# Two layers of Mamba and expert blocks on one core: later low parts, sums in fours, border loads moved

## The chip, the cores and the metric

The kernel runs on one core of a Trainium2 chip. Its time is the device time of one execution in microseconds, the median of several runs. The core has five engines that run side by side, each in its own order: TensorE (PE in the profile; its weight loads are PEld), VectorE (DVE), ScalarE (ACT), GpSimd (POOL) and SyncE (SP), which issues most transfers. They wait for each other through semaphores. PSUM has eight banks of 128 x 512 numbers.

## The reference, cut to what matters

```python
x = L0_attn_x                                  # (8, 256, 128)
xn = layernorm(x)
s = mamba0(xn)                                 # 16 states a channel
g = silu(moe0(xn))                             # 8 experts, the best one for each token
x = x + s * g
xn = layernorm(x)
s = mamba1(xn)                                 # 256 channels, 4 heads, 16 states
g = silu(moe1(xn))                             # all 8 experts for each token, mixed
x = x + s * g

# mamba: h = exp(delta * A) * h + delta * B * u      (a scan over the 256 tokens)
#        y = sum over the 16 states n of h[n] * C[n]
# moe1:  sum over e of cw[e] * (silu(x @ w_gate[e]) * (x @ w_up[e])) @ w_down[e]
```

All of it is in float32.

## The kernel before

The eight sequences are worked on in four pairs; a pair is 512 tokens and fills a PSUM bank's width. Layer 0 runs for all four pairs (0 to 3), then layer 1 for all four. The two layers meet at about 258 us, and this place is called the border here.

**The order of work** is written out by hand in slots. Every pair has 32 slots (UNITS), so layer 0 has slots 0 to 127. Each engine has a function `slot0` (layer 0) and `slot1` (layer 1) that issues what stands in its lists for the slot: `now(LIST, s)` gives the indices whose entry is s. Engines do not meet at slots: each goes through its own list as fast as its waits on semaphores allow, and in order, so that what stands behind a waiting instruction waits too. SyncE goes through the same slots with its transfers.

**A chunk** g of layer 0 is one state n of one pair, 64 in all, 16 a pair. `CH0` gives its slot: every second one in pairs 0 to 2. ScalarE forms its decay four chunks ahead (`decay0`), VectorE multiplies the drive by B (`drive0`, slot CH0) and scans over the tokens (`scan0`, one slot later, four state buffers in a ring), and GpSimd multiplies the state by C (`multiply0`, line 1293; VectorE does the first ten). B and C of a chunk come by one broadcast transfer from a row in memory into one of six places (`load_cb0`, lines 570 to 575), once the product that last read the place is done. TensorE sums the products over the states in a bank: `sum_product` (line 1911) multiplies the product by the identity, one matmul pair each (float32 matmuls are issued as two). `GROUP_OF` (line 104) says how many chunks GpSimd adds up itself before TensorE sums: two in pair 1, else one. In a group the first product goes to its buffer, each further one to `addend`, and an addition (line 1313) puts it on top. At the end of a pair VectorE forms y = x + sum (`tail`, step y, line 935), TensorE transposes it, VectorE takes mean and variance, GpSimd the root, VectorE the shift, ScalarE normalises, TensorE transposes back (step yn) and multiplies by the output weights. These steps stand in the slots 36 to 47 after the pair's start (`DVE_TAIL` and its likes).

**Beside it** in layer 0, 15 blocks of 256 tokens sorted by expert go through moe0 in slots 18 to 81: TensorE turns a block, ScalarE takes it, TensorE multiplies up, ScalarE takes the relu, TensorE multiplies down, ScalarE takes it out, SyncE stores it (`UP_AT` and the lists made from it). GpSimd gathers the weights of a block (`load_pack`) and later the results by token (`fetch`).

**Gate weights of layer 1** are multiplied in three passes of a fast format: for expert e SyncE loads 256 KB into one of two stages (`load_gate`, line 549), ScalarE copies the high part at slot `SPLIT_AT[e]` = 30 + 8e (`split_high`, line 1444), VectorE subtracts to get the low part at `SPLIT_LOW_AT[e]` (`split_low`, line 741). A stage is loaded again once its low part is done, so the load of e waits for low part e-2:

```python
                if e >= 2:
                    sp.wait_ge(wl_ready.sem, wl_ready.at0(0, e - 1))
```

**Layer 1** needs at its start: the mixing weights of each expert, spread over the partitions (`load_cw`, line 612: 256 KB for one expert, in the two halves of `cwb`, which layer 0 uses for a chunk's B and C until chunk 52), with which GpSimd weighs the tokens for the up product (`weigh_tokens`, line 1369); the first four chunks' B and C (`load_cb1`, line 577, two transfers of 256 KB each); and the next pair's tokens (`load_x`, line 563), whose statistics VectorE takes in slot 1 of layer 1, while pair 0 is still being worked on. In `weigh_tokens` of pair 0 and expert 0 GpSimd follows right behind its last product of layer 0. `up1` on TensorE (line 2019) reads the weighed tokens. The last steps of layer 0 on VectorE are the gate of pair 3 (`gate0`, line 958), then the delta of layer 1 (line 885), the first drive and the y of pair 3.

Of the kernel before, what the change touches and what calls it, by code (L numbers as in the profile page):

```python
# [35 lines left out]
PAIRS = B // NB  # L36
TT = T // 128
E, FT = 8, 4
UNITS = E * FT
# [52 lines left out]
XW_SLOT = 30  # L92
SPARED = 4
FIRST_GATES = [125, 127]

CH0 = [UNITS * i + (2 * c if i < PAIRS - 1 else int(1.5 * c)) for i in range(PAIRS) for c in range(N)]
CHUNKS1 = [c if c < 8 else c - 1 for c in range(C1)]
# [3 lines left out]

PLACE = [k % SIX for k in range(UNITS - FT)] + [0, 1, 4, 5]
SUM_LAG1 = 4
GROUP_OF = [2 if i in (1,) else 1 for i in range(PAIRS)]
GROUPS0 = [list(range(N * i + k, N * i + k + GROUP_OF[i])) for i in range(PAIRS) for k in range(0, N, GROUP_OF[i])]
GROUP0 = {g: n for n, group in enumerate(GROUPS0) for g in group}
SUM0_AT = [CH0[group[-1]] + (4 if len(group) > 1 else max(3, 5 - group[0] % N) if group[0] >= N else 3) for group in GROUPS0]
# [25 lines left out]
ROWS_AT = 18  # L133
PACKS = 3
SPLIT_AT = [30 + 8 * e for e in range(E)]
SPLIT_LOW_AT = [at + 4 for at in SPLIT_AT]
GATHER_AT = [80, 88, 96, 115]
TANH_AT = [85, 93, 102, 120]
GATE_AT = [87, 95, 104, 122]
# [26 lines left out]
def cb_before(g):  # L166

    earlier = [n for n in range(min(g, PAIRS * N)) if CB_OF[n] == (CB_OF[g] if g < PAIRS * N else g - PAIRS * N)]
    return earlier[-1] if earlier else None
# [13 lines left out]
def now(slots, u):  # L183

    if isinstance(slots, dict):
        return slots.get(u, "").split()
    return [c for c, at in enumerate(slots) if at == u]
# [111 lines left out]
def build(nc, x, out, x1, crow, cwrow, sorted_in, sorted_out, w):  # L299
    ctx = ExitStack()  # L300
    with ctx:
# [244 lines left out]
        def _(sp):  # L546
            tokens = lambda ap, i: ap[i * T:i * T + T, :].rearrange("(k p) d -> p k d", p=128)

            def load_gate(e):

                if e >= 2:
                    sp.wait_ge(wl_ready.sem, wl_ready.at0(0, e - 1))
                if e == 0:
                    sp.wait_ge(cv_ready.sem, cv_ready.at0(0, 1))
                sp.dma_start(stage[:, e % 2, :], w["Wg"][e]).then_inc(stage_in[e].sem, 16)
# [4 lines left out]
            def load_wu(e):  # L560
                sp.dma_start(wu[:, e, :], w["Wu"][e]).then_inc(wu_in.sem, 16)

            def load_x(j):
                sp.wait_ge(xn_ready.sem, xn_ready.at1(j, 0))
                sp.wait_ge(x_out.sem, x_out.at0(j + 1, 0))
                sp.dma_start(xt[:, :, :], tokens(x1, j)).then_inc(x_in.sem, 16)

            def load_cb0(g):

                if g % N == 0:  # L570
                    sp.wait_ge(rows_out[0].sem, rows_out[0].at0(g // N, 32))
                if cb_before(g) is not None:
                    sp.wait_ge(state_used.sem, state_used.at0(0, cb_before(g) + 1))
                src = crow[(g // N) % 2, 0, g % N:g % N + 1, :, :].rearrange("n k t -> n (k t)")
                sp.dma_start(cb_pair(g).rearrange("p k t -> p (k t)"), src.to_broadcast((128, 2 * T))).then_inc(cb0_in[CB_OF[g]].sem, 16)
# [21 lines left out]
            def load_block(b):  # L597

                if b == 0:
                    for k in range(TT):  # L600
                        sp.wait_ge(scattered[k].sem, scattered[k].at0(0, 16 * PAIRS))
                if b >= 2:
                    sp.wait_ge(blk_turned.sem, blk_turned.at0(0, b - 1))
                src = sorted_in[BLOCK * b:BLOCK * b + BLOCK, :].rearrange("(k p) d -> p k d", p=128)
                sp.dma_start(blk_x[:, b % 2, :, :], src).then_inc(blk_in[b % 2].sem, 16)

            def store_block(b):
                sp.wait_ge(blk_out_ready.sem, blk_out_ready.at0(0, b + 1))
                dst = sorted_out[BLOCK * b:BLOCK * b + BLOCK, :].rearrange("(k p) d -> p k d", p=128)
                sp.dma_start(dst, blk_out[:, b % 2, :, :]).then_inc(blk_out_done[b % 2].sem, 16)  # L610

            def load_cw(j, e):

                if j == 0 and e == 0:
                    sp.wait_ge(state_used.sem, state_used.at0(0, max(g for g in range(PAIRS * N) if CB_OF[g] == ROWS) + 1))
                if j > 0 or e >= CWR:
                    sp.wait_ge(xw_ready.sem, xw_ready.at1(j, e - CWR + 1))
                if e == 0:
                    sp.wait_ge(cw_out.sem, cw_out.at1(j, 16))
                src = cwrow[j % 2, e:e + 1, :].to_broadcast((128, T))  # L620
                sp.dma_start(cwb[:, e % CWR, :], src).then_inc(cw_in[e % CWR].sem, 16)

            def send_cw(j):
                sp.wait_ge(*use1(head_read, j, "cwT"))
                sp.dma_start(cwrow[j % 2, :, :], cwT[:, :]).then_inc(cw_out.sem, 16)
# [31 lines left out]

            for s in range(PAIRS * UNITS):
                i, u = divmod(s, UNITS)
                for e in now(SPLIT_AT, s + 10):  # L660
                    if e >= 2:
                        load_gate(e)
                for g in range(CB_RING, PAIRS * N):
                    if s == CH0[cb_before(g)] + (4 if g < 3 * N else 3):
                        load_cb0(g)
                for b in now(LOAD_AT, s):
                    load_block(b)
                for b in now(STORE_AT, s):
                    store_block(b)
                if u == ROWS_AT and i + 1 < PAIRS:  # L670
                    send_rows(i + 1, 0, 0)
                for step in now(ACT10 if i == PAIRS - 1 else {}, u):
                    if step == "cwT":
                        send_cw(0)
                    if step in ("row0", "row1"):
                        send_rows(0, 1, int(step[3]))
                if s == UP_AT[-1] + 2:
                    load_residual(0, 0)
                for j in now(GATED_AT, s - 3):
                    send_out(j, 0)  # L680
                    load_residual(j + 1, 0)
                if s == GATED_AT[0] + 5:
                    load_x(0)

                for e in range(2, E):
                    if s == 3 * UNITS + 4 + e:
                        load_wu(e)
                if s == GATED_AT[1] + 8:
                    sp.wait_ge(x_out.sem, x_out.at0(2, 0))
                    load_wu(0)  # L690
                    load_wu(1)
                if s == DOWN_AT[-1] + 6:
                    sp.wait_ge(blk_down.sem, blk_down.at0(0, BLOCKS))
                for e in range(E):
                    if s == (DOWN_AT[-1] + 6 + e if e < 6 else 3 * UNITS + 2 + e):
                        if e == 6:
                            sp.wait_ge(yT_ready.sem, yT_ready.at0(3, 0))
                        load_wd(e)
            for i in range(PAIRS):
                last = i == PAIRS - 1  # L700
                if i > 0:
                    load_cw(i, 1)
                for c in range(ROWS):
                    load_cb1(i, c)
                if i == 0:
                    load_cw(0, 0)
                    load_x(1)
                    load_cw(0, 1)
                for u in range(UNITS):
                    if u == LATE + 1 and i + 2 < PAIRS:  # L710
                        load_x(i + 2)
                    if u == (LATE if i else FIRST_LATE):
                        send_out(i - 1 if i else PAIRS - 1, int(i > 0))
                        if i == PAIRS - 1:
                            sp.wait_ge(x_out.sem, x_out.at0(PAIRS, 0))
                        load_residual(i, 1)
                    for step in ([] if last else now(ACT1, u)):
                        if step == "cwT":
                            send_cw(i + 1)
                        if step in ("row0", "row1"):  # L720
                            send_rows(i + 1, 1, int(step[3]))
                    for c in now(CHUNKS1, u - 1):
                        if c + ROWS < C1:
                            load_cb1(i, c + ROWS)
                    if u % FT == 0 and u // FT + CWR < E:
                        load_cw(i, u // FT + CWR)
                    if u == XW_SLOT - 1 and not last:
                        load_cw(i + 1, 0)
# [5 lines left out]
        def _(dve):  # L734
# [234 lines left out]
            def slot0(s):  # L969
# [13 lines left out]
                for k, name in pair_tail(DVE_TAIL, DVE_TAIL_LAST, s):  # L983
                    tail(k, name)
                for e in now(SPLIT_LOW_AT, s):
                    split_low(e)
# [762 lines left out]
        def _(pe):  # L1749
# [228 lines left out]
            def slot0(s):  # L1978
# [5 lines left out]
                for k, name in pair_tail(PE_TAIL, PE_TAIL_LAST, s):  # L1984
                    tail(k, name)
                if s in FIRST_GATES:
                    gate1(0, FIRST_GATES.index(s))
                for b in now(TURN_AT, s):
# [208 lines left out]
```

## Time and profile before

| what | value |
|---|---|
| median of 3 runs | 694.93 us (692.76 to 696.48) |
| the profiled execution, its own time | 695.81 us |
| span of its profile | 694.0 us |
| TensorE busy | 585.4 us (84%) |
| VectorE busy | 575.8 us (83%) |
| GpSimd busy | 532.7 us (77%) |
| ScalarE busy | 456.4 us (66%) |
| granted TensorE clock, mean | 0.963 of 2.4 GHz |
| transfers of SyncE's queue | 130.74 MB, 66.6% of the 16 engines' time |

The span goes from the first to the last instruction; the run's own time holds what lies around it as well. Busy shares are means over stages that have different limits: what bounds a stage is read from the stretches and from the engines' rows in time. In a row in time the bracket gives how long the engine was idle just before, and the instruction whose end released it. Several like instructions in a row are merged into one line with their count.

### The profile page before, as it was taken

How to read it: one execution, taken by the hardware profiler on the slowest of the kernel's cores; microseconds unless marked ns; L12 is line 12 of the kernel's file. 1: busy time of each engine (PE TensorE's matmuls, PEld its weight loads, DVE VectorE, ACT ScalarE, POOL GpSimd, SP SyncE). 2: the span in 40 equal slices, each digit the busy share in tenths (PEclk: the TensorE clock that was granted, in tenths of full speed). 3: DMA queues.
4: the chain of work that ended last, by engine and by line, in shares of the span. 5: the costliest groups of instructions: out<-in, count | busy, mean ns of one | idle time of the engine just before them, and what ended most of it. 6: DMA issues, size and time to landing. Idle time of an engine off the chain costs nothing. (4 is left out here: it accounts for less than half of the span.)

```text
span 694.0 us, 8481 instructions
## 1 busy us (share of the span) xinstructions
PE 585.4 (84%) x2135; PEld 339.7 (49%) x2135; DVE 575.8 (83%) x906; ACT 456.4 (66%) x723; POOL 532.7 (77%) x431
## 2 busy tenths in 40 slices
PE   4656888899745966889999799998799999899997
PEld 2412667786413423544444454444454544566674
DVE  6899819677788987997988979888989788898995
ACT  4655466877834666856787655886765887776660
POOL 3456356785785575988899799999799999799991
PEclk9999899999877988999999999999999999999999
DMA  8096896898796677677557686767676867678870
GB/s 267 17 322 229 291 296 207 286 288 294 218 306 238 224 193 183 177 201 189 153 158 198 177 203 198 189 160 190 175 197 185 208 168 192 173 204 215 221 197 15
DMA packets 71216, 142.25 MB, mean 205 GB/s; under 512 B 8352, under 2 KB 37088, under 8 KB 71168
## 3 DMA queue, kind: packets, MB, share of 16 engines
q1 hardware_dynamic: 67984, 130.74, 66.6%
q0 software_dynamic: 3184, 10.98, 4.7%
q8 instruction: 17, 0.28, 0.2%
q14 instruction: 31, 0.25, 0.1%
HBM read 133.23 MB, written 8.45 MB: 204 GB/s over the span
## 5 line engine op out<-in xcount | busy, mean ns | idle before, releaser
L927 DVE TENSOR_TENSOR_SCAN state<-decay,bank 128x512 f32<-128x512 f32 x128 | 155.9, 1218 | 12.9 <-POOL product L1262 5.3
L2019 PE MATMUL bank<-xw,wu 128*128 128x512 f32 x256 | 133.9, 605 | 14.3 <-DVE hid L1046 11.0
L1262 POOL TENSOR_TENSOR product<-state,CB 128x512 f32<-128x512 f32 x90 | 117.0, 1300 | 16.1 <-DVE state L927 12.3
L1264 POOL TENSOR_TENSOR product<-product 128x512 f32<-128x512 f32 x90 | 119.5, 1328 | 7.1
L1671 ACT ACTIVATE sg<-bank 128x512 f32<-128x512 f32 x128 | 75.4, 597 | 67.4 <-PE bank L1909 58.8
L2037 PE MATMUL bank<-hid,wd 128*128 128x512 f32 x192 | 99.1, 597 | 7.2 <-DVE hid L1046 7.2
L1046 DVE TENSOR_TENSOR hid<-sg,bank 128x512 f32<-128x512 f32 x128 | 85.0, 666 | 22.3 <-PE bank L2019 20.6
L920 DVE TENSOR_TENSOR bank<-bank,CB 128x512 f32<-128x512 f32 x128 | 88.8, 694 | 13.4 <-DMA CB<-crow 11.5
L1921 PE MATMUL bank<-product,early 128*128 128x512 f32 x112 | 71.3, 737 | 32.8 <-POOL product L1307 13.5
L1583 ACT ACTIVATE decay<-delta,negA 128x510 f32<-128x510 f32 x128 | 82.5, 710 | 12.0 <-DVE delta L885 6.8
L1907 PE MATMUL bank<-XH,wh 128*128 128x512 f32 x128 | 74.1, 579 | 9.9 <-ACT sg L1671 3.6
L905 DVE TENSOR_TENSOR_SCAN state<-decay,bank 128x512 f32<-128x512 f32 x64 | 77.9, 1217 | 3.0
L2019 PEld LDWEIGHTS bank<-xw,wu 128*128 128x128 f32 x256 | 45.8, 192 | 64.8 <-issue 46.2
L1307 POOL TENSOR_TENSOR product<-state,CB 128x512 f32<-128x512 f32 x31 | 40.5, 1313 | 22.5 <-DVE state L905 15.7
L1591 ACT ACTIVATE decay<-delta,negA 128x510 f32<-128x510 f32 x64 | 44.9, 714 | 15.4 <-DVE state L905 13.4
L1921 PEld LDWEIGHTS bank<-product,early 128*128 128x128 f32 x112 | 22.5, 228 | 62.9 <-POOL product L1307 26.3
L2037 PEld LDWEIGHTS bank<-hid,wd 128*128 128x128 f32 x192 | 35.1, 189 | 35.7 <-issue 27.2
L1908 PE MATMUL bank<-XL,wh 128*128 128x512 f32 x128 | 50.7, 396 | 0.0
L1909 PE MATMUL bank<-XH,wl 128*128 128x512 f32 x128 | 50.7, 396 | 0.0
L1907 PEld LDWEIGHTS bank<-XH,wh 128*128 128x128 f32 x128 | 24.4, 190 | 38.1 <-ACT sg L1671 13.3
L1583 ACT ACT_TABLE_LOAD x32 | 41.1, 1283 | 0.6
L1371 POOL TENSOR_TENSOR xw<-XR,cwb 128x512 f32<-128x512 f32 x30 | 39.4, 1312 | 2.3 <-PE bank L2019 1.0
(242 smaller groups left out, 1137.3 us busy)
## 6 DMA issues: line engine op xcount, KB each, us to landing
CB<-crow SPq DMA_DIRECT2D x256, 256.0 KB, 4.1
CB<-crow SPq DMA_DIRECT2D x44, 512.0 KB
cwb<-cwrow SPq DMA_DIRECT2D x32, 256.0 KB, 4.7
szm<-crow SPq DMA_DIRECT2D x11, 512.0 KB
cwb<-crow SPq DMA_DIRECT2D x9, 512.0 KB
xw<-Wg_dram SPq DMA_DIRECT2D x8, 256.0 KB, 2.9
wd<-Wd_dram SPq DMA_DIRECT2D x8, 256.0 KB, 5.5
wu<-Wu_dram SPq DMA_DIRECT2D x8, 256.0 KB, 5.3
```

The source lines that it names most:

```text
L905: v.tensor_tensor_scan(state[:, g % RING, :], place0(g), drive, 0.0, ALU.mult, ALU.add).then_inc(state_ready.sem, 1)
L920: v.tensor_tensor(drive, dx, CB[:, c % ROWS, 1, :], ALU.mult).then_inc(drive_ready.sem, 1)
L927: v.tensor_tensor_scan(state[:, c % RING, :], decay[:, PLACE[c], :], drive, 0.0, ALU.mult, ALU.add).then_inc(state_ready.sem, 1)
L1046: v.tensor_tensor(hid[:, u % 2, :], sg[:, PLACE[u], :], bank[up_bank(i, u)][:, :], ALU.mult).then_inc(hid_ready.sem, 1)
L1262: p.tensor_tensor(addend, state[:, c % RING, :], cs, ALU.mult).then_inc(state_used.sem, 1)
L1264: ins = p.tensor_tensor(product[:, m, :], product[:, m, :], addend, ALU.add)
L1583: a.activation(by_batch(decay[:, PLACE[c], :])[:, :, 1:], by_batch(delta[:, m, :])[:, :, 1:], ACT.Exp, scale=negA[:, c:c + 1]).then_inc(de ...
L1671: a.activation(sg[:, PLACE[u], :], bank[stream_bank(u)][:, :], ACT.Silu).then_inc(silu_ready.sem, 1)
L1907: t.matmul(dst, wh[:, e, ws], XH[:, :], start=True, stop=False)
L1921: t.matmul(bank[Y_BANK][:, :], ident[:, :], product[:, PRODUCT_OF[n], :], start=(c == 0), stop=(group[-1] % N == N - 1)).then_inc(summed.s ...
L2019: t.matmul(bank[up_bank(i, u)][:, :], wu[:, e, 128 * f:128 * f + 128], xw[:, e % 2, :], start=True, stop=True).then_inc(up_ps.sem, 1)
L2037: ins = t.matmul(bank[OUT_BANK][:, :], wd[:, u, :], hid[:, u % 2, :], start=(u == 0), stop=(u == UNITS - 1))
```

## The change

Four edits, in lists and in SyncE's program:

- `GROUP_OF` is 4 instead of 2 for pair 1: GpSimd adds four products before TensorE sums them. The slot of a sum is made from the group's last chunk, as before.
- `SPLIT_LOW_AT` is nine slots behind `SPLIT_AT`, for the last expert six, instead of four.
- `load_gate(e)` stands six slots ahead of `SPLIT_AT[e]` instead of ten.
- The border's loads move into the slots of layer 0: `load_x(1)` to slot 96 + 14 = 110, `load_cw(0, 0)` and `load_cw(0, 1)` to slot 96 + 23 = 119. Before, they stood behind the first eight B and C transfers of layer 1.

```diff
+NEXT_X_AT, FIRST_CW_AT = 14, 23
...
-GROUP_OF = [2 if i in (1,) else 1 for i in range(PAIRS)]
+GROUP_OF = [4 if i in (1,) else 1 for i in range(PAIRS)]
...
-SPLIT_LOW_AT = [at + 4 for at in SPLIT_AT]
+SPLIT_LOW_AT = [at + (9 if e < E - 1 else 6) for e, at in enumerate(SPLIT_AT)]
...
             for s in range(PAIRS * UNITS):
                 i, u = divmod(s, UNITS)
-                for e in now(SPLIT_AT, s + 10):
+                for e in now(SPLIT_AT, s + 6):
                     if e >= 2:
                         load_gate(e)
...
                 if s == GATED_AT[0] + 5:
                     load_x(0)
+                if s == 3 * UNITS + NEXT_X_AT:
+                    load_x(1)
+                if s == 3 * UNITS + FIRST_CW_AT:
+                    load_cw(0, 0)
+                    load_cw(0, 1)
...
                 for c in range(ROWS):
                     load_cb1(i, c)
-                if i == 0:
-                    load_cw(0, 0)
-                    load_x(1)
-                    load_cw(0, 1)
```

## Rows read from the trace of the kernel before

**Rows 1.** Busy time by stretch: us, then per engine busy (count), PEclk, DMA share, GB/s.
```profile
99.00:160.00 61.00, 55.72 (x311) 44.83 (x310) 42.90 (x58) 46.17 (x95) 43.03 (x36) 0.94 0.84 273
...
254.00:268.00 14.00, 8.19 (x23) 3.83 (x22) 9.29 (x12) 8.61 (x14) 5.20 (x6) 0.87 0.94 222
...
285.00:370.00 85.00, 79.84 (x245) 41.13 (x244) 73.97 (x97) 62.00 (x88) 76.13 (x60) 1.00 0.69 180
```

**Rows 2.** VectorE in time, 80 to 190 us: start, us, line, operation, [idle before <- releaser].
```profile
96.46 0.69 DVE L741 TENSOR_TENSOR wl<-xw,wh 128x512 fp32r<-128x512 f32 x1 [10.80 <-ACT wh L1444]
...
99.36 0.69 DVE L935 TENSOR_TENSOR xd<-xt,bank 128x512 f32<-128x512 f32 x1 [0.24 <-PE bank L1921]
...
114.54 1.23 DVE L953 SCALAR_TENSOR_TENSOR shift_t<-mv_t,rstd_t 128x4 f32<-128x4 f32 x1 [0.38 <-POOL rstd_t L1190]
...
143.44 1.00 DVE L741 TENSOR_TENSOR wl<-xw,wh 128x512 fp32r<-128x512 f32 x1 [2.61 <-ACT wh L1444]
...
158.76 0.69 DVE L935 TENSOR_TENSOR xd<-xn,bank 128x512 f32<-128x512 f32 x1 [2.83 <-issue]
```

**Rows 3.** TensorE in time, 75 to 160 us, same columns.
```profile
98.30 1.02 PE L1921 MATMUL bank<-product,early 128*128 128x512 f32 x2
...
117.36 1.05 PE L1755 MATMUL bank<-early,wu 128*128 128x128 f32 x4 [2.77 <-ACT wu L1651]
...
137.85 3.68 PE L1810 MATMUL bank<-sg,wd 128*128 128x256 f32 x8 [1.99 <-ACT sg L1600]
...
151.68 1.02 PE L1921 MATMUL bank<-product,early 128*128 128x512 f32 x2
152.54 0.38 PE L1800 MATMUL bank<-early,hid 128*128 128x128 f32 x2
```

**Rows 4.** Who waited for whom on GpSimd, 99 to 160 us: total us, times, longest.
```profile
POOL product L1311 <- DVE state L905: 10.1, 6, 1.8
POOL product L1307 <- DVE state L905: 4.1, 1, 4.1
```

**Rows 5.** GpSimd in time, at the border of the layers.
```profile
254.18 1.26 POOL L1307 TENSOR_TENSOR product<-state,CB 128x512 f32<-128x512 f32 x1
255.40 1.25 POOL L1229 TENSOR_TENSOR sp_x<-sp_x,sp_e 128x512 f32<-128x512 f32 x1
256.62 1.25 POOL L1307 TENSOR_TENSOR product<-state,szm 128x512 f32<-128x512 f32 x1
266.50 1.09 POOL L1369 TENSOR_TENSOR xw<-XNP,cwb 128x512 f32<-128x512 f32 x1 [8.62 <-DMA cwb<-cwrow]
```

**Rows 6.** VectorE: line 958 (min/median/max ns, first and last start), and rows in time after 254 us.
```profile
L958 DVE SCALAR_TENSOR_TENSOR yfT<-yfT,sg x4: 665/768/3991, 189.8 to 254.4; 128x512 f32<-128x512 f32 x4
...
267.08 0.87 DVE L746 BATCH_NORM_STATS2 stats<-xt 128x6 f32<-128x128 f32 x4 [4.04 <-DMA xt<-x]
...
292.73 0.70 DVE L920 TENSOR_TENSOR bank<-bank,CB 128x512 f32<-128x512 f32 x1 [0.70 <-DMA CB<-crow]
...
296.34 0.70 DVE L920 TENSOR_TENSOR bank<-bank,CB 128x512 f32<-128x512 f32 x1 [1.02 <-DMA CB<-crow]
```

**Rows 7.** ScalarE in time, around 145 us and at the border.
```profile
144.99 0.38 ACT L1614 ACTIVATE hid<-bank 128x256 f32<-128x256 f32 x1 [0.52 <-PE bank L1823]
...
259.06 1.33 ACT L1583 ACTIVATE decay<-delta,negA 128x510 f32<-128x510 f32 x2 [4.66 <-DVE delta L885]
```

**Rows 8.** The border on TensorE and SyncE, and one line of the transfers (issue to landing).
```profile
267.64 2.08 PE L2019 MATMUL bank<-xw,wu 128*128 128x512 f32 x2 [3.18 <-POOL xw L1369]
...
249.38 0.32 SPq L625 DMA_DIRECT2D cwrow<-cwT  x1
...
252.85 5.00 SPq L588 DMA_DIRECT2D CB<-crow  x8
257.95 0.53 SPq L621 DMA_DIRECT2D cwb<-cwrow  x1
...
cwb<-cwrow SPq DMA_DIRECT2D x32, 256.0 KB, 4.7
```

## The prediction

> **What bounds the kernel now.** I read four views in this order. First the table of stretches [rows 1]. Between 99 and 160 us, where the second pair of layer 0 runs beside the expert blocks, TensorE is busy 55.72 of 61 us, GpSimd 43.03, VectorE 42.90: TensorE sets the pace and GpSimd has 18 us to spare. From 254 to 268 us, the border of the layers, no engine is busy much over half of the time and the transfer engines are at 0.94. In layer 1 (285 to 370 us) TensorE has 79.84, GpSimd 76.13 and VectorE 73.97 of 85 us: three engines nearly full, so there a head start lasts only if all three have it.
>
> Second, VectorE's order of work [rows 2]. The largest wait is 10.80 us, from 85.66 us on, for the high part of the first gate weights. After it VectorE does one low part, one scan and one drive, is done at 99.36-0.24 = 99.12 us, and still waits 0.24 us for TensorE's sum before it can take the first pair's y. The second wait of this kind, 2.61 us before 143.44 us, is followed by an idle time of 2.83 us before the second pair's y at 158.76 us.
>
> Third, TensorE [rows 3]. It has two waits over half a microsecond in 99 to 160 us: 2.77 us before 117.36 us (for the normalised y of ScalarE) and 1.99 us before 137.85 us (for ScalarE's turned block). One sum takes 0.86 us of it: 151.68 to 152.54 us.
>
> Fourth, the border [rows 5 to 8]. GpSimd ends its last product of layer 0 at 257.88 us and then waits 8.62 us for the mixing weights of the first expert, VectorE waits 4.04 us for the next tokens, TensorE 3.18 us for GpSimd's weighed tokens. SyncE issued the weights at 257.95 us and the tokens right behind, after eight transfers for B and C from 252.85 us on.
>
> **The change, part by part.**
>
> **Low parts later.** Low part e goes from slot 34+8e to 39+8e (92 for the last), the load of gate weights e from slot 20+8e to 24+8e (e from 2 on). Eight subtractions stay eight. Removed are the waits of 10.80 and 2.61 us [rows 2]. But VectorE then reaches the first y early and waits for TensorE's sum until 99.3 us as before: the gain there is at most the 0.24 us between 99.12 and 99.36. What is late next is that sum (slot 33), which hangs on the blocks that TensorE and ScalarE hand to each other. The second wait turns into a longer wait before 158.76 us. So I count both at 0. The cost: low(0) now stands in slot 39 between the variance of the first y and its shift. The low part takes 0.69 us (96.46 us), the slack there is the wait of 0.38 us before 114.54 us [rows 2], so 0.3 us on the chain to ScalarE's normalising and TensorE's transposes at 117.36 us. If a GpSimd addition holds the low part up as well, one GpSimd instruction more, 1.26 us [rows 5]. Bounds 0 and +1.6, and I take +0.3: one addition stood beside this place before, too, and the wait was only 0.38 us. Low(1) to low(3) stay in the pair in which VectorE waits for TensorE anyway, low(4) comes to where low(5) leaves, low(6) and low(7) move within one stretch: 0.
>
> SyncE's queue: the load of gate weights e waits for low part e-2. That wait now stands one slot behind the low part (before: two), and it blocks the load of B and C of a later chunk and a block's load behind it. For e=2 SyncE waits in slot 40 until low(0) of slot 39, which is done before 114.54 us. What stands behind it has its first reader in slot 43 (the block, turned by TensorE just ahead of its wait of 2.77 us) and slot 48 (chunk 24), at 61/32 = 1.9 us a slot 8 and 17 us behind slot 39, and a transfer of 256 KB lands in 4.7 us [rows 8]: hidden by 3 us or more. Without that cover it costs what is late of them. The high part follows its load by six slots, over 11 us: hidden.
>
> **Sums in fours.** Sums at slots 38, 46, 54 and 62 go; those at 42, 50, 58 and 66 stay. Four sums by 0.86 us are 3.4 us of TensorE [rows 3]. The first (slot 38) goes into the wait of 2.77 us behind it, and the second (slot 46) into that of 1.99 us, since ScalarE ends both. The third (slot 54) and the fourth (slot 62, at 151.68 us) stand in a stretch without a wait of TensorE, where ScalarE waits for it by only 0.52 us (144.99 us, [rows 7]) and becomes the later one if TensorE gains more: I count half of each, -0.8. Bounds: 0 (ScalarE holds all) and -3.4 (all four count). GpSimd gets four additions more, 8 to 12, at 1.26 us: 5.0 us. They lie in its 18 us of idle time, of which 10.1 and 4.1 us are waits for VectorE's states [rows 4]. With these additions it still has some 13 us. The last addition of the pair comes before TensorE gets to slot 66, so the y of the pair stays where TensorE puts it. Without that cover the additions cost their 5.0 us (the slower rival).
>
> **Border loads.** Three transfers of 256 KB move up in SyncE's order: the tokens to slot 110, the two weights to slot 119, ahead of the eight B and C transfers. The tokens pass sends and loads of rows; what they read and write was ready some ten slots before. The weights wait for their own row in memory, sent at 249.38 us, and SyncE is at slot 119 at about 252.8 us [rows 8]. They put 512 KB ahead of the first B and C, which at the 222 GB/s of this stretch [rows 1] land some 2.4 us later. If VectorE's first drive of layer 1 has nothing to spare, that is a bound of +2.4.
>
> With the weights in place by about 257.5 us (issue to landing 4.7 us in the median, [rows 8]), GpSimd goes on at 257.9 instead of 266.50 us, TensorE's first up product could start at 267.64-3.18 = 264.46 us, and VectorE saves 4.04 us. By these rows alone TensorE is the last, so -3.2.
>
> Against it stands VectorE's gate instruction, line 958 [rows 6]. All of its operands are in SBUF; it takes 0.67 us at least and 0.77 in the median, but the last one, at 254.4 us, took 3.99 us. It began while GpSimd's product of 254.18 us ran, and two instructions followed that one without a gap (255.40 and 256.62 us, [rows 5]); it ended 0.5 us behind the last, at 258.4. So VectorE did not get in between GpSimd instructions that follow each other at once. In the changed kernel two weighings of 1.09 us follow at once as well, and the gate instruction would end at about 260.5 us: +2.1 on VectorE's delta, on ScalarE's decays, which waited 4.66 us for it (259.06 us, [rows 7]), on its silus and on TensorE's gate products, behind which the first up product stands. 264.46+2.1 = 266.6 us, a gain of 1.1 instead of 3.2. Then GpSimd is no longer six microseconds behind the states; the waits of VectorE of 0.70 and 1.02 us for B and C at 292.73 and 296.34 us [rows 6], whose buffers GpSimd frees, should shrink: -1.0. Border: -2.1, bounds -4.9 (3.2 and both waits of 1.7) and +1.5.
>
> The Trainium skill, "SBUF — State Buffer", section "SBUF: two separate sides", says that VectorE and GpSimd share a pair of ports under an exclusive lock, held for one whole instruction, while the other blocks. The row above agrees that it blocks and goes further, since it lasted over three instructions. By the page's rule taken for one instruction at a time the gate instruction would be let in at 255.4 us, and the border would give the full 3.2; I go by the row.
>
> **Sum.** +0.3 - 0.8 - 2.1 = -2.6 us. The profiled execution took 695.81 us (span 694.0 and 1.8 around it), which gives 693.2; it lies 0.9 above the median of 694.93 us, so a median of 692.3 us. About 0.5%, 3.5 us, is what a measurement of this kernel tells from no change; the forecast lies just inside it.
>
> **Rivals.**
> A. The border gives all: VectorE slips in between, or the weights land just after the gate instruction. 3.2 and 1.7 us at the border, 0.5 to 1 before it: -5.4, 689.5 us. For it: 8.62 us of GpSimd idle at a place where all three later bounds gain. Against: the gate instruction of 3.99 us.
> B. The border gives nothing: B and C come late behind the weights and VectorE is held 2.1 us. 694.9 us.
> C. Slower: GpSimd becomes the bound of the second pair. Place: slots 44 to 64; price: four additions by 1.26, 5.0 us, so 699.9 us. It decides as soon as GpSimd's waits for states [rows 4] are used up, since a state buffer comes free only by its product, which then stands behind an addition. For it: product and addition are 2.5 us a chunk, and chunks come in bursts behind VectorE's waits. Against: 43.03+5.0 = 48 us of work in 61.
> D. The waits of 10.80 and 2.61 us come back in full, as the share of busy time would suggest: -10 or more, 684 us. Against: TensorE's sum at 98.30 us.
> That the move does nothing at all is B.
>
> **Chances.** Forecast (-1 to -4) 0.47, A 0.26, B 0.12, C 0.09, D 0.06. Faster by over 0.5%: A, D and the edge of the forecast, 0.41. Slower by over 0.5%: C, 0.09. Within: 0.50. The range leaves out D and most of C: 687.5 to 697.0. The forecast's own range is 690.9 to 694.
>
> **What would show it.** Right: no wait for wh, but VectorE waiting about 10 us for TensorE's sum before the first y and 5 or more before the second; 52 sums of two matmuls instead of 56; GpSimd's weighing near 258 us; the gate instruction (yfT by yfT and sg) over 5 us long; TensorE's first up product about 1 us earlier against the border's own start. Wrong: a first y well before 99 us (D), a gate instruction under 4 us (A), GpSimd without waits from 117 to 160 us (C), or a drive of chunk 0 of layer 1 waiting for its transfer (B).

## The result, and the profile after

The changed kernel takes 698.88 us in the median of 18 runs (694.47 to 703.2), the kernel before 695.17 us in the runs beside it: a ratio of 1.0053, interval 1.0034 to 1.0072. It is slower, by 3.7 us. The profiled execution took 699.40 us with a span of 697.6 us, 3.6 us over the one before.

The table of stretches of the changed kernel (us, then each engine's busy time and count, granted clock, DMA share, GB/s), against [rows 1]:

```profile
99.00:160.00 61.00, 52.39 (x292) 42.50 (x291) 43.31 (x56) 44.08 (x90) 47.73 (x39) 0.92 0.79 264
254.00:268.00 14.00, 8.47 (x12) 3.17 (x11) 11.01 (x8) 8.20 (x14) 12.00 (x11) 0.65 0.68 176
285.00:370.00 85.00, 78.88 (x242) 40.67 (x242) 73.66 (x96) 61.65 (x91) 76.47 (x60) 1.00 0.71 179
```

In the second pair TensorE is 3.3 us less busy and GpSimd 4.7 us more. That has the direction that the sums in fours ask for, but the sizes can't be read here: the line counts 19 matmuls fewer, and the sums are only 8 of them. The stretches are fixed in time, and the changed kernel runs later in them (its last gate instruction starts at 260.99 us instead of 254.43), so they hold different work, at the border above all. The loss isn't to be read from these lines. Over the whole span VectorE is busy 586.4 us, 10.6 us more than before, with 906 instructions in both kernels: some of them became longer. That alone is no loss either: the changed kernel without its later low parts (e15, e18 below) has 583.8 and 583.2 us and isn't slower than the kernel before. Which instruction became longer, and where, has to be read in time.

VectorE in time, the changed kernel (start, us, line, operation, [idle before <- releaser]; its lines stand two further down than before), against [rows 2]:

```profile
100.12 0.69 DVE L937 TENSOR_TENSOR xd<-xt,bank 128x512 f32<-128x512 f32 x1 [10.04 <-PE bank L1923]
...
111.72 0.68 DVE L743 TENSOR_TENSOR wl<-xw,wh 128x512 fp32r<-128x512 f32 x1
...
115.85 1.23 DVE L955 SCALAR_TENSOR_TENSOR shift_t<-mv_t,rstd_t 128x4 f32<-128x4 f32 x1 [0.33 <-POOL rstd_t L1192]
...
192.48 0.67 DVE L743 TENSOR_TENSOR wl<-xw,wh 128x512 fp32r<-128x512 f32 x1
193.06 1.76 DVE L960 SCALAR_TENSOR_TENSOR yfT<-yfT,sg 128x512 f32<-128x512 f32 x1
...
200.49 3.62 DVE L743 TENSOR_TENSOR wl<-xw,wh 128x512 fp32r<-128x512 f32 x1
...
214.67 3.05 DVE L756 TENSOR_SCALAR veps<-mv 128x4 f32<-128x4 f32 x1
...
221.04 0.68 DVE L937 TENSOR_TENSOR xd<-wd,bank 128x512 f32<-128x512 f32 x1
...
260.99 5.03 DVE L960 SCALAR_TENSOR_TENSOR yfT<-yfT,sg 128x512 f32<-128x512 f32 x1 [1.56 <-ACT yfT L1623]
```

GpSimd in time, the same kernel, in the third pair and at the border:

```profile
198.88 0.94 POOL L1226 DMA_INDIRECT sg<-sorted_out,slot_of  x1 [0.30 <-issue]
199.83 1.28 POOL L1309 TENSOR_TENSOR product<-state,CB 128x512 f32<-128x512 f32 x1
201.06 1.27 POOL L1352 TENSOR_TENSOR wu<-wu,xr 128x512 f32<-128x512 f32 x1
202.28 1.27 POOL L1309 TENSOR_TENSOR product<-state,CB 128x512 f32<-128x512 f32 x1
205.31 1.27 POOL L1309 TENSOR_TENSOR product<-state,cwb 128x512 f32<-128x512 f32 x1 [1.77 <-DVE state L907]
...
260.73 1.25 POOL L1309 TENSOR_TENSOR product<-state,CB 128x512 f32<-128x512 f32 x1
261.94 1.25 POOL L1231 TENSOR_TENSOR sp_x<-sp_x,sp_e 128x512 f32<-128x512 f32 x1
263.16 1.25 POOL L1309 TENSOR_TENSOR product<-state,szm 128x512 f32<-128x512 f32 x1
264.38 1.08 POOL L1371 TENSOR_TENSOR xw<-XNP,cwb 128x512 f32<-128x512 f32 x1
266.42 1.16 POOL L1371 TENSOR_TENSOR xw<-XNP,cwb 128x512 f32<-128x512 f32 x1 [0.95 <-DMA cwb<-cwrow]
```

The last low part, low(7), begins at 200.49 us inside a run of three GpSimd instructions without a gap (199.83, 201.06, 202.28 us, the last ends at 203.55) and ends at 204.11: 3.62 us instead of 0.68. The run has its gap only because GpSimd's next product waits 1.77 us (the row of 205.31 us) for a state whose scan stands behind low(7) on VectorE; before, five instructions followed each other there. Some ten microseconds later the input variance (line 756) meets the next run of the same kind. Before the change low(7) stood beside gathers, and the whole of it (194.46 to 195.14 us) lies within one of them:

```profile
193.03 0.95 POOL L1224 DMA_INDIRECT sg<-sorted_out,slot_of  x1 [0.30 <-issue]
194.28 0.94 POOL L1224 DMA_INDIRECT sg<-sorted_out,slot_of  x1 [0.30 <-issue]
```

VectorE of the kernel before, same stretch:

```profile
194.46 0.68 DVE L741 TENSOR_TENSOR wl<-xw,wh 128x512 fp32r<-128x512 f32 x1
...
202.33 0.87 DVE L958 SCALAR_TENSOR_TENSOR yfT<-yfT,sg 128x512 f32<-128x512 f32 x1 [1.77 <-ACT yfT L1621]
...
208.69 0.87 DVE L746 BATCH_NORM_STATS2 stats<-xt 128x6 f32<-128x128 f32 x4 [1.12 <-DMA xt<-x]
...
211.16 1.04 DVE L754 TENSOR_SCALAR veps<-mv 128x4 f32<-128x4 f32 x1
...
215.52 0.68 DVE L935 TENSOR_TENSOR xd<-wd,bank 128x512 f32<-128x512 f32 x1
```

Longer by the change: low(7) 2.94, the variance 2.01, the gate at 193.06 us 1.1 (0.67 before). Against that, the waits of 1.77 and 1.12 us are used up. That leaves about 3 us, and the third pair's y comes 59.67 us behind the second's instead of 56.76. Not all of it is low(7)'s: the gate takes 1.76 us in every kernel with low(6) in slot 87, and the variance takes 1.03 to 2.04 us in the kernels with low(7) in slot 90, so the 1.04 us before is the low end.

**The stages.** I cut every profile at the start of each pair's y on VectorE (line 935 or 937), and at its first `hid` of layer 1 (line 1046 or 1048). For the two kernels, in us:

| stage | before | after | difference |
|---|---|---|---|
| start to first y | 99.36 | 100.12 | +0.8 |
| first to second y | 59.40 | 61.25 | +1.9 |
| second to third y | 56.76 | 59.67 | +2.9 |
| third y to first hid | 54.24 | 52.66 | -1.6 |
| first hid to the end | 424.2 | 423.9 | -0.3 |

The differences add up to the 3.6 us but for rounding. One profile's stage scatters by 1 to 3 us; with twenty profiles of kernels that have or lack an edit, the groups below tell more than one pair does.

### The profile page after: what moved, and what is told of

Read it like the earlier page. It is cut to its first block and busy times, and to the rows that moved or that the text cites. A ratio compares the mean times of both kernels' runs of the same rounds, so it can differ in the third digit from the quotient of the medians.

```text
span 697.6 us, 8472 instructions
## 1 busy us (share of the span) xinstructions
PE 586.1 (84%) x2127; PEld 339.5 (49%) x2127; DVE 586.4 (84%) x906; ACT 456.4 (65%) x723; POOL 540.3 (77%) x435
## 5 line engine op out<-in xcount | busy, mean ns | idle before, releaser
L2021 PE MATMUL bank<-xw,wu 128*128 128x512 f32 x256 | 132.1, 598 | 13.8 <-DVE hid L1048 13.8
L1264 POOL TENSOR_TENSOR product<-state,CB 128x512 f32<-128x512 f32 x90 | 117.9, 1310 | 17.6 <-DVE state L929 13.8
L1309 POOL TENSOR_TENSOR product<-state,CB 128x512 f32<-128x512 f32 x28 | 36.6, 1312 | 18.2 <-DVE state L907 11.0
```

What stands on the lines that cost most here:

```text
L1264: p.tensor_tensor(addend, state[:, c % RING, :], cs, ALU.mult).then_inc(state_used.sem, 1)
L2021: t.matmul(bank[up_bank(i, u)][:, :], wu[:, e, 128 * f:128 * f + 128], xw[:, e % 2, :], start=True, stop=True).then_inc(up_ps.sem, 1)
```

## The experiments

The ratios are against the kernel before, with their intervals:

| kernel | ratio | interval |
|---|---|---|
| e1 border alone | 0.9989 | 0.9968 to 1.0010 |
| e2 fours alone | 1.0015 | 0.9997 to 1.0032 |
| e3 low parts and load offset alone | 1.0077 | 1.0046 to 1.0107 |
| e4 border and fours | 0.9996 | 0.9979 to 1.0013 |
| e5 changed kernel, low(7) back | 1.0020 | 1.0002 to 1.0038 |
| e6 changed kernel, block load ahead | 1.0072 | 1.0045 to 1.0099 |
| e7 border, low(0) to low(5) late | 1.0031 | 1.0015 to 1.0046 |
| e8 border, gap on GpSimd | 0.9994 | 0.9977 to 1.0010 |
| e9 low(7) alone | 1.0025 | 1.0003 to 1.0047 |
| e10 load offset alone | 0.9992 | 0.9975 to 1.0008 |
| e11 low(0) | 1.0008 | 0.9987 to 1.0029 |
| e12 low(1) to low(6) | 1.0024 | 1.0004 to 1.0043 |
| e13 low(1) to low(5) | 0.9997 | 0.9979 to 1.0016 |
| e14 low(6) | 0.9999 | 0.9977 to 1.0020 |
| e15 changed kernel, all low parts back | 0.9979 | 0.9959 to 1.0000 |
| e16 low(0) to low(5) | 1.0009 | 0.9991 to 1.0028 |
| e17 low(6) and low(7) | 1.0043 | 1.0026 to 1.0060 |
| e18 as e15 | 0.9993 | 0.9975 to 1.0010 |

**One edit at a time: e1 to e4.** Each takes its lines of the change and leaves the rest as before; e4 takes two edits.

e1, the border:

```diff
+                if s == 3 * UNITS + NEXT_X_AT:
+                    load_x(1)
+                if s == 3 * UNITS + FIRST_CW_AT:
+                    load_cw(0, 0)
+                    load_cw(0, 1)
...
-                if i == 0:
-                    load_cw(0, 0)
-                    load_x(1)
-                    load_cw(0, 1)
```

> Only the border loads move; the rest is the kernel before. Theory L (the low parts and their loads made the changed kernel slower, the border gained): 1 to 3 us faster than before, gate instruction of line 958 about 5 us long, layer 0 up to that instruction as before (254 to 255 us). Rival F (the border costs, VectorE being held behind GpSimd): slower by 1 us or more.

e2, the fours:

```diff
-GROUP_OF = [2 if i in (1,) else 1 for i in range(PAIRS)]
+GROUP_OF = [4 if i in (1,) else 1 for i in range(PAIRS)]
```

> Only the sums in fours. Theory L: within 1.5 us of before, TensorE continuous from 138 us on, second y at 158 to 159.5 us. Rival G (GpSimd's additions made it slower): 2.5 to 5 us slower, second y at 161 us or later.

e3, the low parts with their loads:

```diff
-SPLIT_LOW_AT = [at + 4 for at in SPLIT_AT]
+SPLIT_LOW_AT = [at + (9 if e < E - 1 else 6) for e, at in enumerate(SPLIT_AT)]
...
-                for e in now(SPLIT_AT, s + 10):
+                for e in now(SPLIT_AT, s + 6):
```

> Only the low parts nine slots behind and the gate loads six slots ahead. Theory L: 4 to 7 us slower than before; the shift of the first y about 1 us later, TensorE waiting for a block's load at about 115 to 119 us, a low part or another SBUF instruction of VectorE held for 3 us or so near 200 us. Rival G or F: within 1.5 us of before.

e4, the diffs of e1 and e2 together:

> Border loads and sums in fours, low parts as before. Theory L: 1 to 4 us faster than before, so 5 to 8 us faster than the changed kernel. Rival G: 0 to 4 us slower than before.

The low parts alone cost 5.4 us (1.0077), at least as much as the whole change (the intervals overlap). The border is at 0.9989, the fours at 1.0015, both at 0.9996: neither can be told from no change by its time, and the 1 us or more that I expected of the border (e1, e4) isn't seen. In e1 the gate instruction took 3.98 us, not the 5 that I expected. So the loss is the edit whose moves I had counted at +0.3 us.

**The hold of low(7): e5 and e9.** e5 is the changed kernel with low(7) back in slot 90:

```diff
-SPLIT_LOW_AT = [at + (9 if e < E - 1 else 6) for e, at in enumerate(SPLIT_AT)]
+SPLIT_LOW_AT = [at + (9 if e < E - 1 else 4) for e, at in enumerate(SPLIT_AT)]
```

> The changed kernel with the last low part alone back in slot 90. Theory S (the low part of slot 92 starts while GpSimd instructions follow each other without a gap, is held 3 us, and the variance near 214 us is held after it): no low part near 195 to 201 us above 1 us, the third pair (second y to third y) shorter by 2 to 3.5 us than in the changed kernel's 59.7 us, median 695.5 to 697. Rival O (the late low parts cost by their place in VectorE's order, each a little): within 1 us of the changed kernel.

e9 is the reverse, the kernel before with low(7) alone in slot 92:

```diff
-SPLIT_LOW_AT = [at + 4 for at in SPLIT_AT]
+SPLIT_LOW_AT = [at + (4 if e < E - 1 else 6) for e, at in enumerate(SPLIT_AT)]
```

> The kernel before with one low part moved alone: low(7) from slot 90 to slot 92. Theory L (the last low part, put where GpSimd's instructions follow without a gap, carries most of the loss): wl near 199 us takes 3.6 us instead of 0.68, the variance behind it over 2.5 us, and the ratio to the kernel before is 1.004 to 1.006. Rival S (the low parts cost as a sum over all eight, none alone): a ratio of 1.000 to 1.002.

e5 loses 0.20% where the changed kernel loses 0.53%, and e9 loses 0.25%, less than the 0.4 to 0.6% that I expected. One subtraction two slots later costs some 2 us: over half of the changed kernel's 3.7, under half of the 5.4 of e3. In e9 the hold is there, on VectorE

```profile
195.61 4.15 DVE L741 TENSOR_TENSOR wl<-xw,wh 128x512 fp32r<-128x512 f32 x1
...
210.33 3.06 DVE L754 TENSOR_SCALAR veps<-mv 128x4 f32<-128x4 f32 x1
```

beside this run on GpSimd:

```profile
195.51 1.27 POOL L1307 TENSOR_TENSOR product<-state,CB 128x512 f32<-128x512 f32 x1
196.73 1.26 POOL L1350 TENSOR_TENSOR wu<-wu,xr 128x512 f32<-128x512 f32 x1
197.95 1.25 POOL L1307 TENSOR_TENSOR product<-state,CB 128x512 f32<-128x512 f32 x1
200.97 1.27 POOL L1307 TENSOR_TENSOR product<-state,cwb 128x512 f32<-128x512 f32 x1 [1.77 <-DVE state L905]
```

**SyncE's queue: e6 and e10.** In the changed kernel TensorE waits 3.95 us, until 119.09 us, for a block that SyncE loaded behind a held load of gate weights. e6 puts that load behind the block's:

```diff
-                for e in now(SPLIT_AT, s + 6):
-                    if e >= 2:
-                        load_gate(e)
...
                 for b in now(STORE_AT, s):
                     store_block(b)
+                for e in now(SPLIT_AT, s + 6):
+                    if e >= 2:
+                        load_gate(e)
```

> The changed kernel with the load of gate weights behind the chunk's and the block's transfers of its slot in SyncE's order. Theory Q (that load's wait held up the block's load, and TensorE waited 3.95 us for it): no wait of TensorE for a block above 0.5 us near 115 us, first y to second y 1 to 2 us shorter than 61.25 us, median 1 to 2 us below the changed kernel. Rival: TensorE waits as long for ScalarE's normalised y instead, no difference above 0.5 us.

TensorE in time, the changed kernel:

```profile
119.09 0.69 PE L1802 MATMUL bank<-early,hid 128*128 128x128 f32 x2 [3.95 <-DMA hid<-sorted_in]
119.56 1.06 PE L1757 MATMUL bank<-early,wu 128*128 128x128 f32 x4
```

and e6:

```profile
116.13 0.38 PE L1802 MATMUL bank<-early,hid 128*128 128x128 f32 x2
119.81 1.11 PE L1757 MATMUL bank<-early,wu 128*128 128x128 f32 x4 [3.30 <-ACT wu L1653]
```

The block's turn runs at once, and TensorE then waits 3.30 us for ScalarE's normalised y, as it did before the change [rows 3]. The time is 1.0072, no better. The wait of 3.95 us is real, and no cost of it shows in the time. In the rows it costs little: the matmul behind it (line 1757) comes 19.44 us behind the first y in the changed kernel and 18.53 in e6, and in the five other kernels with a late low(0), where TensorE waits 2.49 to 3.04 us for its block, it comes at 18.52 to 18.55.

e10 is the offset of the loads alone (`s + 10` to `s + 6`):

> The kernel before with the loads of the gate weights six slots ahead of the high parts instead of ten, low parts unmoved. Theory L: the later loads alone cost nothing, ratio 0.999 to 1.001. Rival Q (the loads' place in SyncE's queue costs: B and C behind them land later, or the high part waits for its weights): a ratio of 1.002 or more, with waits of ScalarE for xw or of VectorE for CB in the rows.

0.9992: nothing.

**Which of the others: e7, and e11 to e14, e16, e17.** All but e7 are the kernel before with the loads six slots ahead and this list of lags; e7 has the border as well.

```diff
-SPLIT_LOW_AT = [at + 4 for at in SPLIT_AT]
+SPLIT_LOW_AT = [at + (9 if e < 6 else 4) for e, at in enumerate(SPLIT_AT)]
```

(e7 and e16; e11 has `e < 1`, e13 `1 <= e < 6`, e14 `e == 6` as its condition, e12 `4 if e < 1 or e > 6 else 9`, and e17 `4 if e < 6 else 9 if e == 6 else 6`.)

> Border loads, low parts nine slots behind for experts 0 to 5 and four behind for 6 and 7, no sums in fours. Theory S: third pair as before (56.5 to 57.5 us), median 691 to 694, 1 to 4 us faster than before. Rival O: 696 or more.

> The kernel before with low(0) nine slots behind its high part, loads six slots ahead, all other low parts unmoved. Theory L: VectorE waits about 10 us for TensorE's sum instead of for wh, SyncE is held at slot 40; the ratio is 0.999 to 1.002. Rival Z (the low part between variance and shift is what e5 and e7 still lose): 1.002 to 1.004.

> The kernel before with low(1) to low(6) nine slots behind their high parts, loads six slots ahead; low(0) and low(7) unmoved. Theory L: the rest of the loss is low(3), low(1) and gate(0) held by GpSimd (2.3 to 3.4 us instead of 1.0): a ratio of 1.001 to 1.004. Rival Z (the rest is low(0)): 0.999 to 1.001.

> The kernel before with low(1) to low(5) nine slots behind their high parts, loads six slots ahead; low(0), low(6) and low(7) unmoved. Theory M (the cost of the middle low parts lies in the second pair, where low(1) was held 2.4 us at 121 us and low(3) up to 3.4 at 148): a ratio of 1.001 to 1.003. Rival N (it is low(6) in slot 87, ahead of the gate): 0.999 to 1.001.

> The kernel before with low(6) alone nine slots behind its high part (slot 87, the slot of the gate), loads six slots ahead. Theory M: wl and the gate behind it together cost 1 us at most more, hidden before the pair's y: 0.999 to 1.001. Rival N: the gate held 1.8 us and the third pair's y over 1 us later against the second's: 1.001 to 1.003.

> The kernel before with low(0) to low(5) nine slots behind, loads six slots ahead; low(6) and low(7) unmoved; no fours, no border. Each of low(0) and low(1) to low(5) alone cost nothing (1.0008 and 0.9997). If they cost together what the kernel with them and the border seemed to lose (1.0031 against 0.9989): a ratio of 1.003 or more. Rival (holds in the second pair are covered by VectorE's waits there, together as well): 0.999 to 1.002.

> The kernel before with low(6) in slot 87 and low(7) in slot 92, loads six slots ahead; low(0) to low(5) unmoved; no fours, no border. Theory P (the loss is made in the third pair, where VectorE is held in a stretch without waits of its own): 1.004 to 1.008, y1 to y2 59 us or more against 56.8. Rival (it needs the low parts of the second pair as well): 1.001 to 1.003.

Low(1) to low(5) move together in all of these. e13 gives the sharpest contrast. VectorE in time, e13:

```profile
147.16 3.40 DVE L741 TENSOR_TENSOR wl<-xw,wh 128x512 fp32r<-128x512 f32 x1
...
157.53 0.69 DVE L935 TENSOR_TENSOR xd<-xn,bank 128x512 f32<-128x512 f32 x1 [1.34 <-PE bank L1921]
```

Low(3) is held 3.40 us, as long as low(7) in the changed kernel, and the kernel is at 0.9997: behind it VectorE still waits 1.34 us for TensorE's sum, so the hold is covered. Low(0) to low(5) together (e16), with low(1) held for 2.42 and low(3) for 3.43 us in that stretch, are at 1.0009. Low(6) and low(7), in the third pair, are at 1.0043 with 59.47 us from the second to the third y. So the place decides: a hold counts where VectorE's waits behind it, before the pair's y, are shorter than what it adds. In the third pair they were 1.77 and 1.12 us, and the hold used them up. No run keeps low(7) in slot 92 and gives GpSimd a gap there, so how much of the cost is the hold and how much the new place in VectorE's order is read from the rows, not tested.

**What low(7) leaves open.** The earlier low parts cost something too, and the runs don't say where. With and without a late low(0) to low(5) the ratios are 1.0077 and 1.0043 (e3, e17) and 1.0031 and 0.9989 (e7, e1, of which e7 has the load offset too); with and without a late low(0) to low(6) 1.0020 and, in two measurements, 0.9979 and 0.9993 (e5; e15, e18). Each pair differs by 0.3 to 0.4%, 2 to 3 us. e12 (1.0024) leans the same way, while e16 (1.0009), e13 and e14 show next to nothing; e7 missed the 691 to 694 us that I expected with 696.26. The profiles don't show it: the third y comes at 215.74 us in the mean of the seven kernels with some of low(0) to low(6) late and low(7) in slot 90, and at 215.72 in the eight with none late. The place of these 2 us or so stays open.

**Without any moved low part: e15 and e18.** The changed kernel with `SPLIT_LOW_AT` at four slots again, the same kernel twice:

```diff
-SPLIT_LOW_AT = [at + (9 if e < E - 1 else 6) for e, at in enumerate(SPLIT_AT)]
+SPLIT_LOW_AT = [at + 4 for e, at in enumerate(SPLIT_AT)]
```

> The changed kernel with all eight low parts back at four slots behind their high parts; fours, the loads' place and the border stay. If the low parts are all of the loss: 0.997 to 1.000 against the kernel before, and y1 to y2 near 56.6 us in the profile. Rival (the edits cost together what none costs alone): 1.002 or more.

> The same kernel as e15, once more, since it is the only one under the kernel before: 0.996 to 1.000 if its gain is real, over 1.000 if it was chance.

0.9979 and 0.9993: this kernel is 0.5% and more under the changed one in both, so the low parts are the whole loss. It may be 0.1% under the kernel before; neither that nor a lead over e1, e4 and e8 is shown.

**The border's hold: e8.** The border edit alone, with GpSimd waiting for the gate before its last product of layer 0:

```diff
                 for g in now(CH0, s - 1):
+                    if g == PAIRS * N - 1:
+                        pool.wait_ge(g_ready.sem, g_ready.at0(PAIRS - 1, 1))
                     if g >= FIRST_DVE:
                         multiply0(g)
```

> Border loads only, and GpSimd's last product of layer 0 waits for VectorE's gate instruction. If VectorE is held only because GpSimd's instructions follow without a gap: the gate instruction takes 2 to 3 us instead of 4, VectorE's delta starts 1 us earlier against it, and the time is 0 to 1.5 us below that with the border loads alone. If it is held by something else: still about 4 us.

VectorE in time, e8:

```profile
255.17 2.77 DVE L960 SCALAR_TENSOR_TENSOR yfT<-yfT,sg 128x512 f32<-128x512 f32 x1 [1.56 <-ACT yfT L1625]
```

and GpSimd in time beside it:

```profile
254.91 1.25 POOL L1309 TENSOR_TENSOR product<-state,CB 128x512 f32<-128x512 f32 x1
256.13 1.25 POOL L1231 TENSOR_TENSOR sp_x<-sp_x,sp_e 128x512 f32<-128x512 f32 x1
258.02 1.65 POOL L1309 TENSOR_TENSOR product<-state,szm 128x512 f32<-128x512 f32 x1 [0.63 <-DVE yfT L960]
```

With a gap made by hand the gate ends 0.6 us behind the instruction before the gap (2.77 us instead of 3.98 in e1, 5.03 in the changed kernel). That ties the hold to the absence of a gap. The time stays at 0.9994, not under e1 as I expected, and third y to first hid is 54.09 us. What VectorE gained at the gate it waited away at its first drive of layer 1, for B and C:

```profile
258.57 1.65 DVE L893 TENSOR_TENSOR bank<-delta,xs 128x512 f32<-128x512 f32 x1
263.25 0.70 DVE L922 TENSOR_TENSOR bank<-bank,CB 128x512 f32<-128x512 f32 x1 [3.02 <-DMA CB<-crow]
```

## Why the prediction was wrong

Forecast 692.3 us, range 687.5 to 697.0, slower at 0.09; it came to 698.88. The rival that stood for slower (C, GpSimd the bound of the second pair) isn't what happened: e2 alone is at 1.0015, and GpSimd in the changed kernel still waits for VectorE's states in this stretch:

```profile
POOL product L1313 <- DVE state L907: 8.6, 4, 5.9
```

That is 8.6 us against 14.2 [rows 4].

**The step that failed** is "low(6) and low(7) move within one stretch: 0". I took one stretch for one price. By e17 these two moves are 1.0043, 3.0 us, and the stage in which they lie says the same: in the five profiles with low(7) in slot 92 the third y comes 58.87 to 60.82 us behind the second (mean 59.67), in the fifteen others 56.35 to 57.47 (mean 56.74). The two groups don't overlap. The means are 2.9 us apart. In the times low(7) alone is 1.7 us (e9) or 2.3 (the changed kernel against e5). I had the mechanism in hand: I read that VectorE did not get in between GpSimd instructions without a gap, and used it for low(0) and for the border's gate [rows 5, 6], but not for the slot to which low(7) was moved. The row to ask for was GpSimd's order around slot 92, and it was there before: 196.50 to 202.65 us, five instructions, no gap.

**Low(0) between variance and shift, +0.3.** Right in kind, and 0.5 in size. It took 0.68 us; in the seven profiles with a late low(0) the shift comes 15.7 us behind the first y, in the thirteen others 15.2. e11 is at 1.0008. The same cost was overlooked for low(4), which "comes to where low(5) leaves" at 0. It comes to slot 71 and not to low(5)'s 74, and there stands between the variance and the shift of the second y (169.40 and 173.18 us in the changed kernel): that shift comes 11.8 us behind its y in the eight profiles with a late low(4), 11.3 in the others. Whether the time pays for it isn't shown. The mean of the second y over the seven profiles with a late low(0) is 159.20 us, over the thirteen others 159.07. The 61.25 us between the first two in the changed kernel's own profile is the longest of the twenty, and the other six with a late low(0) have 57.79 to 58.70: that +1.9 of the table is scatter, or I can't tell it from scatter.

**The waits of 10.80 and 2.61 us, at 0.** Right: the first y waits 10.04 us for TensorE's sum, as forecast, and rival D fell. The wait before the second y is 3.55 us, not the 5 or more that I gave as a sign.

**SyncE's queue, "hidden by 3 us or more".** Wrong in the row: TensorE waited 3.95 us for the block. No price of it shows in the time; in e6 a wait of 3.30 us for ScalarE takes its place.

**Fours, -0.8.** The line of the sums counts 104 matmuls instead of 112 (52 sums instead of 56). In the stages the second y comes at 158.58 us with fours (mean of four profiles with low(0) unmoved) and at 159.29 without (nine): -0.7, the size forecast, but single profiles in each group lie up to 1.8 us from its mean. The times of e2 and e4 don't show it, so it isn't confirmed.

**Border, -2.1.** Partly right. GpSimd weighed the tokens right behind its last product, at 264.38 us, and the gate instruction took 5.03 us. But of the eight profiles with this edit (e8 aside) only this one and e15 show it over 5 us; the six others have 3.97 or 3.98, as before. And the +2.4 for B and C behind the weights was given as a bound and left out of the sum: VectorE's first drive of layer 1 waits for them in six of the eight, 0.26 to 3.15 us, the sign of rival B, and in the two others (e1, e18) the weighings hold the instructions ahead of it. From the gate's start to this drive it is 7.0 to 8.5 us in the eight and 5.4 in each of the eleven without the edit. From the third y to the first hid it takes 52.32 us with the border edit (mean of eight profiles) and 53.94 without (eleven), e8 aside: -1.6, where 3.2 less 2.1 gives -1.1. The times of e1 and e4 don't confirm it. The further -1.0 for VectorE's waits for B and C failed: from there to the end the means are 424.3 and 424.0 us. A head start at the border isn't carried further in layer 1.

The Trainium skill, "SBUF — State Buffer", section "SBUF: two separate sides", has the lock held for one instruction. By that low(7) would have been let in behind the product of 199.83 us and, as an estimate from the rows, have ended near 202 us. Here it ended at 204.11 us, so the row decides again: it lasted until GpSimd had a gap.

With low(6) and low(7) at the 3.0 us of e17 the sum of the parts would have been +0.4 instead of -2.6; with all low parts at the 5.4 us of e3 it would have been +2.5, where 3.7 was measured.

## What to carry to other kernels

Before an instruction of VectorE with all of its operands in SBUF is moved, read GpSimd's order in time at the new place. A run of gapless instructions there prices the move, and the number of slots doesn't: two slots for low(7) made its stage 2.9 us longer, five for low(6) not visibly (57.05 us in e14). Then look how much VectorE waits before the next thing that someone waits for: where 1.34 us were still left, a hold of 3.4 us cost nothing that shows (e13), and where the waits were used up, 3.6 us and the holds beside it cost about 3 (e17). Busy time that grows with no instruction added says that instructions became longer; it doesn't say that time was lost (e15).

## What the hardware showed that I had not expected

One VectorE instruction is held over three or four gapless GpSimd instructions (3.62, 4.15 and 5.03 us, against 0.68), and it isn't the large ones alone: the variance's last step, on 128x4 numbers, took 3.05 us against 0.17 elsewhere in the same kernel. VectorE's scans and drives, which read one of their operands from a PSUM bank, went through beside the same runs at their usual length, as this scan beside GpSimd's products of 187.37 and 188.59 us in the changed kernel:

```profile
187.66 1.22 DVE L907 TENSOR_TENSOR_SCAN state<-decay,bank 128x512 f32<-128x512 f32 x1
```

A result in a bank didn't help where both inputs lay in SBUF: `bank<-delta,xs` of the border takes 0.70 us in the kernel before and 1.48 beside a weighing in e1.

And a gather on GpSimd held low(7) up by nothing: in the kernel before it lies wholly within one (from 194.28 us, 0.94 long) and took 0.68 us.
